# Scan layers: the diagonals of B made by DMA through a DRAM buffer, and the products of delta and x made on DVE instead of POOL

## The reference

```python
def step(h, inp):
    d_t, x_t, b_t, c_t = inp
    h = jnp.exp(d_t[..., None] * A) * h + (d_t * x_t)[..., None] * b_t[:, None, :]
    y_t = jnp.einsum('bdn,bn->bd', h, c_t)
    return (h, y_t)
...
return y + x_in * D
```

## Time and profile before

| | |
|---|---|
| median of 3 runs | 4304.23 us |
| the profiled execution's span, first to last instruction | 4308.6 us |
| scan stage, 32 passes | from about 1722 us to the end |
| one pass (between the same DMA of two passes) | 77.6 us |
| PE, DVE, ACT, POOL busy over the span | 86%, 80%, 49%, 62% |
| DMA in the scan stage: mean rate, share of 16 engines | 104 GB/s, 46% |

### The profile page before, as it was taken

One profiled execution on the slowest core, in us unless ns is written; L12 is line 12 of the kernel. 1 busy time (PEld: TensorE's weight loads), 2 busy tenths in 40 slices (PEclk: granted clock), 3 DMA queues, 4 the chain that ended last, 5 costly groups with the idle time before them and its releaser, 6 DMA issues.

```text
span 4308.6 us, 119610 instructions
## 1 busy us (share of the span) xinstructions
PE 3710.7 (86%) x49136; PEld 2266.0 (53%) x49136; DVE 3432.3 (80%) x3492; ACT 2105.8 (49%) x2803; POOL 2659.4 (62%) x973
## 2 busy tenths in 40 slices
PE   4994899899999996789889888899898888888897
PEld 4994666666666664344444444444444444444443
DVE  6564567667576663699998998999999989999997
ACT  2331343444444443556555555555565555555563
POOL 1111121111211210599899999999999999999998
PEclk9997899999999998799999999999999999999999
DMA  9624142242332330553543543544535535435433
GB/s 101 85 44 108 54 124 81 85 119 70 95 109 69 105 91 25 120 116 79 125 106 83 125 102 92 125 94 103 122 84 120 112 79 124 109 79 130 103 87 83
DMA packets 296948, 416.40 MB, mean 97 GB/s; under 512 B 31369, under 2 KB 185741, under 8 KB 296385
## 3 DMA queue, kind: packets, MB, share of 16 engines
q1 hardware_dynamic: 295440, 408.35, 41.7%
q10 hardware_dynamic: 978, 0.34, 0.0%
HBM read 267.09 MB, written 91.16 MB: 83 GB/s over the span
## 4 chain that ended last, share of the span: by engine, by line
PE 27%; DVE 16%; issue 12%; ACT 3%; POOL 1%; DVEq 1%; DMA 0%; ACTq 0%; POOLq 0%
DVE ssm_h L1136 11%; PE ssm_u_ps L818 10%; PE ssm_y_ps L831 10%; PE ssm_scratch L848 4%; DVE ssm_b_diag L1160 3%; PE ssm_scratch L858 1%; DVE ssm_stats L1143 1%; POOL ssm_h L1216 1%; ACT ssm_decay L967 1%; PE ssm_u_ps L893 1%; DVE ssm_y_sb L1165 1%; ACT ssm_xn L994 1%; PE ssm_scratch L873 1%; PE ssm_scratch L867 0%; DVEq L1128 0%
## 5 line engine op out<-in xcount | busy, mean ns | idle before, releaser
L1216 POOL TENSOR_TENSOR ssm_h<-ssm_h,ssm_c_rep 128x2048 f32<-128x2048 f32 x384 | 1745.4, 4550 | 107.3 <-DVE ssm_h L1136 99.6
L967 ACT ACTIVATE ssm_decay<-ssm_delta_rep,ssm_a_neg 128x1024 f32<-128x1024 f32 x768 | 863.7, 1145 | 592.1 <-DVE ssm_h L1136 589.3
L818 PE MATMUL ssm_u_ps<-ssm_b_diag,ssm_dx_t 64*64 64x128 f32 x24576 | 865.7, 282 | 262.3 <-DVE ssm_h L1136 182.6
L818 PEld LDWEIGHTS ssm_u_ps<-ssm_b_diag,ssm_dx_t 64*64 64x64 f32 x24576 | 696.3, 137 | 698.9 <-issue 694.6
L1136 DVE TENSOR_TENSOR_SCAN ssm_h<-ssm_decay,ssm_h,ssm_u_ps 128x512 f32<-128x512 f32 x768 | 944.3, 1257 | 132.5 <-PE ssm_u_ps L818 131.4
L1136 DVE TENSOR_TENSOR_SCAN ssm_h<-ssm_decay,ssm_u_ps 128x512 f32<-128x512 f32 x768 | 887.2, 1195 | 35.8 <-ACT ssm_decay L967 16.9
L831 PE MATMUL ssm_y_ps<-ssm_h,ssm_state_sum 128*64 128x512 f32 x3072 | 798.1, 643 | 8.0 <-POOL ssm_h L1216 8.0
L1752 ACT ACTIVATE l_probs<-l_work 128x532 f32<-128x532 f32 (+1 forms) x384 | 217.6, 567 | 560.7 <-PE l_work L1606 554.0
L1160 DVE TENSOR_TENSOR ssm_b_diag<-ssm_b_t,ssm_lane 128x2048 f32<-128x2048 f32 x128 | 454.0, 3549 | 22.7 <-ACT ssm_b_t L1022 22.7
L2004 POOL TENSOR_TENSOR l_rstd<-l_var_eps,l_minus_half 96x2 f32<-96x2 f32 x16 | 11.1, 695 | 586.6 <-DVE l_var_eps L1841 586.6
L831 PEld LDWEIGHTS ssm_y_ps<-ssm_h,ssm_state_sum 128*64 128x64 f32 x3072 | 196.8, 144 | 326.3 <-issue 311.9
(11 more groups left out here) (163 smaller groups left out, 5554.7 us busy)
## 6 DMA issues: line engine op xcount, KB each, us to landing
ssm_c_rep<-ssm_c_by_state SPq DMA_DIRECT2D x256, 512.0 KB, 6.5
ssm_delta_rep<-ssm_delta SPq DMA_DIRECT2D x384, 128.0 KB, 5.9
l_qk_parts<-l_qk SPq DMA_DIRECT2D x48, 768.0 KB, 4.8
ssm_x<-x_after_l SPq DMA_DIRECT2D x32, 768.0 KB, 5.8
ssm_x_res<-x_after_l SPq DMA_DIRECT2D x192, 128.0 KB, 4.3
l_x<-x SPq DMA_DIRECT2D x64, 192.0 KB, 9.1
x_after_l<-l_x SPq DMA_DIRECT2D x64, 192.0 KB, 4.1
l_x<-x_after_l SPq DMA_DIRECT2D x16, 768.0 KB, 5.5
```

The source lines that it names most:

```text
L818: made = nc.tensor.matmul(u_ps[64 * par:64 * par + 64, ring("u", w), r, at:at + 128], dx_t[rows, db, 2 * win + k, 64 * g:64 * g + 64], b_d ...
L967: nc.scalar.activation(decay[:, 2 * (s % 2) + npi, :], delta_rep[:, db, :], ACT.Exp, scale=a_neg[:, n.layer, col:col + 1]).then_inc(decay_ ...
L1216: nc.gpsimd.tensor_tensor(view, view, c_rep[:, 2 * q:2 * q + 2, :], ALU.mult).then_inc(c_applied, 1)
```

## The change

- B's diagonals no longer come from DVE. SP stores `b_t` into a DRAM buffer `b_diagonals`, in 8 DMAs a pass (`store_diagonals`, pieces of two float32), and loads the four parts of `b_diag` from it, 2 DMAs of 512 KB each a part (`load_diagonals`). Rows of the buffer are written 2050 numbers apart and read 2048 apart, so that row j's pair lands at column 2j: the off-diagonal zeros are in the buffer already.
- The zeros are written once, by one DMA of 4.2 MB in the attention layer (`diag_cleared`), from a new constant.
- `make_dx` goes from POOL to DVE: after the scans of windows 0 and 4 for blocks 1 and 2, and of window 18 for the next pass's block 0.
- In `late(n)` the order on SP changes. The constant `lane` and its load go.

```diff
+                def store_diagonals(n):
+
+                    await_drained(sp, fill(n, "bt"))
+                    for npq in range(4):
+                        for r in range(2):
+                            b = b_t[64 * r:64 * r + 64, :].rearrange("p (c m) -> p c m", c=16)[:, :, 2 * npq:2 * npq + 2]
+                            sp.dma_start(by_diagonal[npq, r, :, 0:DIAG_ROW].rearrange("j (c x) -> j c x", c=16)[:, :, 0:2],
+                                         b).then_inc(diag_stored, 16)
+
+                def load_diagonals(n, npq):
+
+                    if npq == 0:
+                        sp.wait_ge(diag_stored, n.count(128, 128))
+                        sp.sem_inc(diag_store_seen, 1)
+                    if not n.first:
+                        sp.wait_ge(u_filled, n.count(8 * S_STEPS, 8 * (npq - 3)))
+                    for r in range(2):
+                        sp.dma_start(b_diag[64 * r:64 * r + 64, npq].rearrange("p c a m -> p (c a m)"),
+                                     by_row[npq, r]).then_inc(diag_loaded[npq], 16)
...
                     load_delta(n, 0)
                     store_c(n)
+                    store_diagonals(n)
                     sp.wait_ge(c_stored, 32)
                     load_c(n, 0)
+                    for npq in range(4):
+                        load_diagonals(n, npq)
                     load_c(n, 1)
...
                         store_c(m)
                         load_delta(m, 0)
+                        store_diagonals(m)
+                        sp.wait_ge(decay_made, n.count(TILES_S, 16))
+                        sp.sem_inc(rep_free, 1)
+                        load_delta(m, 1)
+                        load_diagonals(m, 0)
                         sp.wait_ge(c_stored, m.count(32, 32))
                         sp.sem_inc(c_store_seen, 1)
                         load_c(m, 0)
-                        sp.wait_ge(decay_made, n.count(TILES_S, 16))
-                        sp.sem_inc(rep_free, 1)
-                        load_delta(m, 1)
+                        load_diagonals(m, 1)
                         load_c(m, 1)
+                        load_diagonals(m, 2)
+                        load_diagonals(m, 3)
...
-                        pe.wait_ge(diag_made, n.count(4, npq + 1))
+                        pe.wait_ge(diag_loaded[npq], n.count(32, 32))
...
                     scan(n, w // 2, w % 2, 0)
-                    if w in (17, 19, 21, 23) and not last:
-                        diagonals(after(n), w // 2 - 8)
                     scan(n, w // 2, w % 2, 1)
                     if w == 3 and not n.first:
                         keep_y(before(n), 2)
+                    if w in ((3, 8) if n.first else (0, 4)):
+                        make_dx(n, 1 if w < 4 else 2)
+                    if w == 18 and not last:
+                        make_dx(after(n), 0)
```

More of the change, by code:

```diff
@@ L580, in ssm_layers @@
         dx_made = sem("dx_made")
-        diag_made = sem("diag_made")
+        diag_stored = sem("diag_stored")
+        diag_store_seen = sem("diag_store_seen")
+        diag_loaded = [sem(f"diag_loaded{npq}") for npq in range(4)]
         rows_seen = sem("rows_seen")
@@ L1151, in channel_moments, with make_dx @@
                     last.then_inc(moments_made, 1)
[L1153 to L1161, removed]
+                def make_dx(n, db):
+                    dve.wait_ge(delta_made, n.count(3, db + 1))
+                    await_drained(dve, fill(n, f"x.{db}"))
+                    if db:
+                        await_fill(dve, fill(n, f"dx.{db - 1}"))
+                    elif not n.first:
+                        await_fill(dve, fill(before(n), "dx.2"))
+                    for w in range(2):
+                        made = nc.vector.tensor_tensor(by_lane(dx[:, :], w), in_order(x_kept[:, :], w), in_order(delta[:, db, :], w), ALU.mult)
+                    made.then_inc(dx_made, 1)
                 def keep_y(n, db):
@@ L1175, in prologue @@
                     nc.vector.tensor_scalar(a_neg[:, :, :], a_neg[:, :, :], -1.0, None, ALU.mult).then_inc(consts_made, 1)
-                    for npq in range(4):
-                        diagonals(n, npq)
+                    make_dx(n, 0)
                 def window(n, w):
@@ L1226, in finish_delta @@
                     nc.gpsimd.tensor_tensor(delta[:, db, :], relu[:, :], delta[:, db, :], ALU.add).then_inc(delta_made, 1)
-                def make_dx(n, db):
-                    pool.wait_ge(delta_made, n.count(3, db + 1))
-                    await_drained(pool, fill(n, f"x.{db}"))
-                    if db:
-                        await_fill(pool, fill(n, f"dx.{db - 1}"))
-                    elif not n.first:
-                        await_fill(pool, fill(before(n), "dx.2"))
-                    for w in range(2):
-                        made = nc.gpsimd.tensor_tensor(by_lane(dx[:, :], w), in_order(x_kept[:, :], w), in_order(delta[:, db, :], w), ALU.mult)
-                    made.then_inc(dx_made, 1)
                 def add_residual(n, q):
@@ L1253, in step @@
                         finish_delta(n, 1 if s == 0 else 2)
-                    if n.first and s in (1, 4):
-                        make_dx(n, 1 if s == 1 else 2)
                     apply_c(n, s)
-                    if s == 0 and not n.first:
-                        make_dx(n, 2)
                     if s == 1 and not last:
@@ L1560, in main, with tail @@
                         move_rows(n)
-                schedule(sp, prologue, main, store)
+                    if n.first:
+                        sp.dma_start(diag_dram.rearrange("n r k -> (n r) k"),
+                                     consts["zeros"].to_broadcast([8, 64 * (DIAG_ROW + 2)])).then_inc(diag_cleared, 16)
+                def tail(n_next):
+                    store(n_next)
+                    sp.wait_ge(diag_cleared, 16)
+                schedule(sp, prologue, main, tail)
             @block.tensor
```

22 lines of the change are left out of this document (11 added, 11 removed).

## The result

The changed kernel takes **4833.1 us** (median of 4 runs, 4814.3 to 4841.3) where the kernel before took 4303.5 us (4300.5 to 4306.7): ratio 1.122, 95% interval 1.120 to 1.124. Forecast were 4623 us, between 4340 and 4920, slower with a chance of 0.81. Sign and range hold, and the size was too small by 210 us.

The account below looks back on a forecast made before the run. SP's loop of issues, stores, loads and POOL's tail was taken to bound a pass at 87.5 us against 77.6. 4308.6 + 31 x 9.9 (307) + 12 = 4628, less 4.4: 4623 us, range 4340 to 4920.

Parts of the forecast that it names:

- SP's loop: From POOL's last residual sum through SP's issues, stores, loads and POOL's last steps: 87.5 us a pass against 77.6.
- 1 SP's issues: Residual stores and loads, x, C stores and `delta_rep` on SP, ahead of the stores of diagonals: 14.9 us.
- 2 stores, to the first load: Eight stores of diagonals, 8192 packets of 8 bytes, 9.1 us plus 2.3 us landing: 11.4 us.
- 3 + 4 start and stream: After the stores, 1.9 us until loads run, then 37.3 us for the loads of diagonals and C.
- 5 POOL's tail: After the last C load, POOL's steps 3 to 6 with three residual sums: 22.0 us.
- the rival of the dear stores: 8-byte stores dearer than 512-byte packets: 4917 us with stores at 20.9 us, 5500 at twice 18.6; chance 0.14.
- step 4: The load stream of a pass: eight pairs of 1.05 MB, diagonals and C, at 225 GB/s, 37.3 us.
- 12 us for the start: At the scan stage's start, stores and first loads after `b_t` delay C's last pair: some 12 us lost.
- The zeros: One 4.2 MB DMA in the attention layer, costed at nothing; up to 20 us, once, if cover is short.
- Engines bound the pass: Rival: transfers are hidden and engines bound the scan pass at 71 us, 4111 us in all; chance 0.13.
- The double lock: Rival: each DVE product pair waits for POOL twice, 7.5 us a pair, 4421 us in all; chance 0.09.
- PE slowing down: After a wait PE's eight matmuls for the sum of states take 3.25 us instead of 1.94; left at nothing.

Follow-up runs that it names:

- e3: The changed kernel with the stores of diagonals in the first pass alone, loads kept in every pass: 4558.6 us, ratio 1.058.
- e5: The changed kernel with the loads of diagonals in the first pass alone, stores kept in every pass: 4296.1 us, ratio 0.997.
- e6: The changed kernel with neither stores nor loads of diagonals after the first pass, products on DVE: 4244.0 us, ratio 0.985.
- e9: The changed kernel itself, run again unedited beside the kernel before, on a third chip: 4908.0 us, ratio 1.139.
- e12: The changed kernel with diagonals stored and loaded in the first pass alone and `make_dx` back on POOL: 4076.2 us, ratio 0.946.
- e2: The kernel before with only `make_dx` moved to DVE, which still makes the diagonals: 4581.4 us, ratio 1.063.
- e8: The changed kernel with four stores of 128 partitions, zeros as 512 rows, and SP's order turned round, stores of diagonals first: 4896.5 us, ratio 1.135.
- e7: The changed kernel with four stores of 128 partitions instead of eight of 64, and zeros written as 512 rows: 4910.3 us, ratio 1.139.

## Why the prediction was right, and where it was short

**What bounds the kernel.** The reading of SP's loop as what closes a pass was right, and e3, e5, e6 and e9 show it: beside the other, each transfer costs its whole length, 18.6 and 11.1 us, and alone only what is over the room of 9.2.

**The terms of the pass**, each against its measurement in one pass:

| term | forecast | measured |
|---|---|---|
| 1 SP's issues | 14.9 | 14.8 |
| 2 stores, to the first load | 11.4 | 12.6 (mean 12.1; 14.1 in e9) |
| 3 + 4 start and stream | 1.9 + 37.3 | 41.8 |
| 5 POOL's tail | 22.0 | 23.4 |
| pass | 87.5 | 92.6 (mean 94.9) |

*The stores* were sized well by the packet rate of the earlier trace rows: 8192 packets in 7.9 us in that run, 9.5 in e9, against my 9.1. The rate of that row, of packets not quite so small, carried over. The upper end, 18.6 us, by the bytes of 512, was wrong by a factor of two. The Trainium skill's least size for full rate ("DMA: Bandwidth & Descriptors", Specifications) holds here in bytes: all queues together move 31 GB/s in the 10 us of the stores. As a price for each packet it was cheaper than a packet of 512 bytes, so the rival of the dear stores did not come.

```profile
DMA packets 8826, 0.31 MB, mean 31 GB/s; under 512 B 8343, under 2 KB 8826, under 8 KB 8826
```

*The stream* was mis-sized: step 4 counted eight pairs and left out the third `delta_rep`, 0.5 MB that SP issues from 3034.83 on, in the midst of them. At the measured 222 GB/s that is 2.4 us of the 2.6 missing. The rate itself, 225, was right.

*The tail* has 1.4 us in which POOL waits for scans.

*One pass or the mean.* I took a clean pass of 77.6 us as the pass of before; the mean is 79.1. The mean of after is likewise 2.3 us over the pass laid out above. Both together make 0.8 us a pass.

The shortfall against the span is 522 - 319 = 203 us: the loop 31 x 15.7 = 488 instead of 307 and 12 (the start lies within the 488), which is 169 (31 x 5.1 from the terms above, the rest from the mean, less the start's 12), the zeros 23, the last pass 11. Of the terms the stream is the largest, 31 x 2.6 = 81 us.

Of the signs that I named, SP's wait of 6 us behind its last store of diagonals, the DMA share over 0.95 for 35 us and the pair of products (0.7 to 3.5 us, where I had said 1 to 4) came about as said; POOL is at 66% instead of 70, and the pass missed its 85 to 90 us.

**At the ends.** I gave 12 us for the start; the first pass alone is 29.5 longer than before, 14 more than a later one, so that term holds. The last pass adds 11, which I had not counted. *The zeros* I costed at nothing, with "up to 20 us, once" if the cover is short. It was short, and cost 19 at the queue and 23 by the first store of C (12 to 16 by the start of the scan stage in the other runs with the same zeros): the idle time of the queue in that batch isn't where the zeros lie, and the very next DMA was one that the batch needs at once.

**Engines bound the pass** (0.13) was wrong twice: the loop does not open, and e6 shows that with products on DVE the pass would have stopped at 76.9 us, not 71. I had put DVE at 68 us there with 3.0 us for a pair; the pair was right (3.2 in e6), and what I missed is that no engine has to be full for that: in 1200 us of e6 PE is busy 1098, DVE 1094 and POOL 991. With the products back on POOL (e12) PE and POOL reach 96% and 95%, so the rest was lost where DVE and POOL hold each other up. **The double lock** (0.09) did not happen as described: no pair came near 7.5 us (the longest in the changed kernel is 3.5 us, the longest single instruction 3.1). Its end, a pass longer than before with hidden DMAs, is what e2 shows where the diagonals stay on DVE, not here. **PE slowing down** after a wait was left at nothing. It is there (3.30 us for 1.94, at a granted clock of 0.50), while the stream still runs, and no run tells its share of the rest.

## What to carry to other kernels

What a transfer costs when it is tried alone is its length less the room that its chain has beside the work, and two transfers in one chain have that room only once: 9.4 and 1.9 us alone, 20.5 together, 18.6 and 11.1 each when the other is there. Look whether a chain of stores, loads and the last work of a pass closes on itself before counting what an engine saves. Move an operation only after asking which engine it will then exclude; price both halves of a change alone and together, and in the state that the other half leaves behind. And sum against the mean pass, from the first and last of a row that occurs once a pass, not against one that looks clean.

## What the hardware showed that was not expected

DMA packets of 8 bytes from SBUF to DRAM went through at some 1030 a microsecond in one run and 860 in another (8192 in 7.9 and 9.5 us), while those of 8 KB took the same in both; with 32 x 8192 of them in a kernel the difference is 50 us by itself (32 x 1.55), of the 75 us between two measurements of the same code (63, 31 x 2.0, by the time from store to load), where the code without them differs by 5. What runs on another chip needs its own run of both kernels. And SP's issue of a DMA is not a constant: it is 0.65 us for `delta_rep`, and behind the tiny packets two stores of C took 5.49 us (e8) instead of 1.31, and four stores of 2048 packets each 5.06 (e7).
